# A two-stage graph kernel: the order of a round is rewritten, and the score row is spread through DRAM instead of by TensorE transposes

## The reference

```python
h = maximum(layernorm(x), 0)                    # h0
# stage L0: attention over the adjacency, K = 3 hops
Xw = h @ Wv + bv
e = leaky_relu((Xw @ aw[:d])[:, None, :] + (Xw @ aw[d:])[:, :, None] + ab, 0.2)
alpha = adj * exp(e);  T = alpha / (alpha.sum(-1) + 1e-12)
H = sum over k of (T^k h) @ Wk[k] + bk[k];   x = x + relu(H)
h = maximum(layernorm(x), 0)                    # h1
# stage L1: three graph convolutions
h = relu(adj @ (h @ W1) + b1);  h = relu(adj @ (h @ W2) + b2)
x = x + adj @ (h @ W3) + b3
```

## Time and profile before

| | |
|---|---|
| median of 3 runs (lowest, highest) | 836.76 us (836.75, 837.14) |
| the profiled execution: its time, its span | 837.53 us, 835.4 us |
| busy: PE, DVE, ACT, POOL | 818.7, 718.0, 684.0, 506.8 us |
| share of the span | 98%, 86%, 82%, 61% |
| mean granted TensorE clock | 0.997 |
| DMA moved | 77.54 MB, mean 93 GB/s |

### The profile page before, as it was taken

One profiled execution on the slowest core, in us unless ns is written; L12 is line 12 of the kernel. 1 busy time (PEld: TensorE's weight loads), 2 busy tenths in 40 slices (PEclk: granted clock), 3 DMA queues, 4 the chain that ended last, 5 costly groups with the idle time before them and its releaser, 6 DMA issues.

```text
span 835.4 us, 20996 instructions
## 1 busy us (share of the span) xinstructions
PE 818.7 (98%) x6219; PEld 772.0 (92%) x6219; DVE 718.0 (86%) x2001; ACT 684.0 (82%) x1673; POOL 506.8 (61%) x591
## 2 busy tenths in 40 slices
PE   7899999999999999999999999999999999999996
PEld 6799999999999999999999999999999999999995
DVE  6989889888889889889889889889888889889882
ACT  4788888888888888888888888888888888888774
POOL 3475665665665665665665665665665665665553
PEclk9999999999999999999999999999999999999999
DMA  7144334334344334334334334334334344344101
GB/s 195 43 99 107 86 95 103 91 94 104 88 95 102 92 93 103 92 93 110 84 93 108 87 93 106 87 94 106 88 94 105 85 97 109 83 95 102 46 27 38
DMA packets 245064, 77.54 MB, mean 93 GB/s; under 512 B 202324, under 2 KB 237016, under 8 KB 244952
## 3 DMA queue, kind: packets, MB, share of 16 engines
q1 hardware_dynamic: 243864, 75.16, 37.5%
q10 hardware_dynamic: 1088, 1.05, 0.4%
HBM read 43.39 MB, written 32.77 MB: 91 GB/s over the span
## 4 chain that ended last, share of the span: by engine, by line
PE 95%; ACT 1%; DVE 1%; DMA 1%; issue 1%; POOL 1%; ACTq 0%; DVEq 0%; POOLq 0%
PE bank L984 44%; PE bank_p L984 37%; PE bank_turned L984 7%; PE bank_T L984 5%; PE bank_T L1003 2%; DMA w_raw<-in_L_gnn_Wk 1%; POOL w_p_lo L422 0%; ACT y_full L614 0%; ACT h L490 0%; POOL y__lo L392 0%; PE bank_p L1160 0%; ACT y__hi L614 0%; DVE stats L693 0%; DVE alpha L766 0%; ACT y_hi L569 0%
## 5 line engine op out<-in xcount | busy, mean ns | idle before, releaser
L392 POOL TENSOR_TENSOR y__lo<-y_full,y__hi 128x256 fp32r<-128x256 f32 x256 | 183.6, 737 | 131.4 <-ACT y_full L614 131.4
L383 POOL TENSOR_TENSOR rstd<-veps,minus_half 128x2 f32<-128x2 f32 x128 | 111.6, 872 | 184.9 <-DVE veps L710 184.9
L984 PE MATMUL bank_p<-w_p_hi,h0T_hi 128*128 128x258 f32 (+1 forms) x512 | 176.3, 361 | 0.2 <-DVE y_full L795 0.2
L984 PE MATMUL bank_p<-w_p_lo,h0T_hi 128*128 128x258 f32 (+1 forms) x512 | 165.7, 339 | 0.0
L984 PE MATMUL bank_p<-w_p_hi,h0T_lo 128*128 128x258 f32 (+1 forms) x512 | 142.5, 340 | 0.0
L984 PE MATMUL bank<-w_gcn_hi,y__hi 128*128 128x256 f32 x512 | 130.2, 290 | 2.1 <-ACT y__hi L614 1.3
L984 PE MATMUL bank<-w_gcn_lo,y__hi 128*128 128x256 f32 x512 | 123.7, 278 | 0.0
L614 ACT ACTIVATE y__hi<-bank,bias_col 128x256 fp32r<-128x256 f32 x256 | 119.9, 468 | 3.6 <-PE bank L984 3.5
L614 ACT ACTIVATE y_full<-bank,bias_col 128x256 f32<-128x256 f32 x256 | 120.6, 471 | 0.0
L984 PEld LDWEIGHTS bank_p<-w_p_hi,h0T_hi 128*128 128x128 f32 x512 | 97.1, 190 | 6.5 <-issue 0.4
L984 PEld LDWEIGHTS bank_p<-w_p_lo,h0T_hi 128*128 128x128 f32 x512 | 97.6, 191 | 6.0
(11 more groups left out here) (100 smaller groups left out, 2285.4 us busy)
## 6 DMA issues: line engine op xcount, KB each, us to landing
x_in<-in_x SPq DMA_DIRECT2D x64, 256.0 KB, 3.0
x_new<-x_out SPq DMA_DIRECT2D x64, 256.0 KB, 2.2
h_rows<-h SPq DMA_DIRECT2D x61, 256.0 KB, 2.0
h_blocks<-h_rows SPq DMA_DIRECT2D x244, 64.0 KB, 2.6
adj_blocks<-in_adj SPq DMA_DIRECT2D x256, 32.0 KB, 2.0
w_raw<-in_L_gnn_Wk ACTq DMA_DIRECT2D x3, 256.0 KB, 6.9
w_raw<-in_L_gnn_W SPq DMA_DIRECT2D x3, 256.0 KB, 3.5
wv_raw<-in_L_gnn_Wv ACTq DMA_DIRECT2D x1, 256.0 KB, 3.8
```

The source lines that it names most:

```text
L383: pool.tensor_tensor(rstd[n][k % 2][:], veps[n][k % 2][:], minus_half[:], ALU.pow)\
L392: pool.tensor_tensor(y[n][1][:, c], y_full[n][:, c], plain(y[n][0][:, c]), ALU.subtract)\
L984: return pe.matmul(dst, stationary, moving, start=start, stop=stop, skip_group_check=True)
```

## The change

The score row no longer goes over TensorE from round 3 on. SP writes column v of `uv` (4 bytes from each partition and graph, 1 KB in all) to a DRAM row, waits until it has landed, and reads the row back broadcast to 128 partitions (128 KB) into `v_bc`, from which ACT makes the logits. Both DMAs stand at the head of SP's round. All five engines' rounds are written in a new order. On TensorE: p2, ay, z1, z3, p0/p1 of graph 0, s2, p0/p1 of graph 1, z2, m, ap, s3; z1 of a pair thus moves over the round's border. The dummy transposes of the drain rounds are gone. `y1_made` is now signalled per graph, s2 and s3 wait for their low halves chunk by chunk.

```diff
+        v_rows = [nc.dram_tensor(f"v_rows{k}", (G, P), F32, kind="Internal").ap() for k in range(2)]
+        v_bc = slots(2, "v_bc", [P, G, P])
...
+            def write_scores(i, k):
+
+                sp.wait_ge(uv_made, i + 1)
+                if i >= SPREAD_ON_TENSOR + 2:
+                    sp.wait_ge(v_landed[k % 2], scores_seen(i - 2))
+                sp.dma_start(v_rows[k % 2].rearrange("g (n o) -> n g o", o=1), uv[k % 2][:, :, 1:2],
+                             allow_slow_non_contiguous=True).then_inc(v_out[k % 2], 16)
+
+            def read_scores(i, k):
+
+                sp.wait_ge(v_out[k % 2], scores_seen(i))
+                if i >= SPREAD_ON_TENSOR + 2:
+                    sp.wait_ge(z_made, i - 1)
+                sp.dma_start(v_bc[k % 2][:], v_rows[k % 2].rearrange("(o g) n -> o g n", o=1)
+                             .to_broadcast([P, G, P])).then_inc(v_landed[k % 2], 16)
...
+                spread = here(i, 0) if i >= SPREAD_ON_TENSOR else None
                 if second(i):
                     load_adj_blocks(3, 3)
-                if turned is not None:
+                if spread is not None:
+                    write_scores(i, k)
+                    read_scores(i, k)
+                if second(i):
                     write_rows(turned, turned % ROUND)
                 if (n := here(i, -2)) is not None and not second(i):
-                    load_adj_blocks(n, n % ROUND)
+                    load_adj_blocks(n, n % ROUND, range(2))
+                if turned is not None and not second(i):
+                    write_rows(turned, turned % ROUND)
+                if (n := here(i, -2)) is not None and not second(i):
+                    load_adj_blocks(n, n % ROUND, range(2, P // SQUARE))
+                if (n := here(i, -4)) is not None and after(i, 1):
+                    load_x(n)
...
+                if b is not None and after(i, 3):
+                    pool.wait_ge(y1_lo, b + 1)
+                    adjT_low(b, (k - LAG_B) % ROUND)
+                if c is not None and after(i, 4) and not tail(i):
+                    out_bias(c, (k - LAG_C) % ROUND)
                 if c is not None:
                     y_low(0, c, k - LAG_C)
...
             def logits(i, k):
 
-                act.wait_ge(spread_done, i + 1)
+                if i < SPREAD_ON_TENSOR:
+                    act.wait_ge(spread_done, i + 1)
+                else:
+                    act.wait_ge(v_landed[k % 2], scores_seen(i))
                 act.wait_ge(uv_made, i + 1)
                 if after(i, 2):
                     act.wait_ge(exp_made, i - 1)
                 for g in range(G):
-                    last = act.activation(z[k % 2][:, g, :], spread_ps[:, g, :], ACT.Prelu,
+                    last = act.activation(z[k % 2][:, g, :], (spread_ps if i < SPREAD_ON_TENSOR else v_bc[k % 2])[:, g, :],
+                                          ACT.Prelu,
                                           bias=uv[k % 2][:, g, 0:1], alpha=SLOPE)
                 last.then_inc(z_made, 1)
 
...
+                if b is not None:
+                    y1_high(b, kb)
...
+                if d is not None:
+                    s3_high(d)
...
+                if (n := here(i, -1)) is not None and n > ON_TENSOR + 1:
+                    hT_high(n, n % ROUND)
...
+                if a is not None and a >= SPREAD_ON_TENSOR:
+                    logits(a, k)
+                    exponentials(a, k)
+                if c is not None:
+                    s2_copy(c)
...
                 for g in range(G):
-                    last = dve.scalar_tensor_tensor(y1_full[k % 2][:, g, :], p2_ps[:, g, :],
-                                                    rinv[k % 2][:, g:g + 1], p1[k % 2][:, g, :],
-                                                    ALU.mult, ALU.add)
-                last.then_inc(y1_made, 1)
+                    dve.scalar_tensor_tensor(y1_full[k % 2][:, g, :], p2_ps[:, g, :],
+                                             rinv[k % 2][:, g:g + 1], p1[k % 2][:, g, :],
+                                             ALU.mult, ALU.add).then_inc(y1_made, 1)
 
...
+                if c is not None and after(i, 3):
+                    m_low(c)
+                if b is not None and after(b, 1):
+                    y1_low(b, kb)
...
+                if b is not None:
+                    p0_bias(b, kb)
+                if d is not None and after(d, 1):
+                    s3_low(d)
...
                 if a is not None:
                     attention(a, k)
+                if d is not None:
+                    finish(d, kd)
+                if a is not None and after(i, 2):
+                    p2_low(a, k)
...
-                pe.wait_ge(y1_lo, i + 1)
-                pe.wait_ge(z_made, i + 1)
-                for g in range(G):
-                    for a, b in PARTS:
+                pe.wait_ge(y1_hi, i + 1)
+                pe.wait_ge(z_made, min(i + 1, SPREAD_ON_TENSOR))
+                if after(i, 1):
+                    pe.wait_ge(h_made, i)
+                for a, b in ((HI, HI), (LO, HI), (HI, LO)):
+                    if b == LO:
+                        pe.wait_ge(y1_lo, i + 1)
+                    for g in range(G):
                         last = matmul(ay_ps[:, g, :], aT[k % 2][a][:, g, :], y1[k % 2][b][:, g, :],
-                                      g == 0 and (a, b) == (HI, HI), a == LO)
+                                      g == 0 and (a, b) == (HI, HI), b == LO)
                 last.then_inc(ay_done, 1)
 
             def aggregate(dst, src, i, k):
...
+            def low_by_chunk(n, i, w, dst):
+
+                for c in range(C):
+                    pe.wait_ge(y_lo[n], C * i + c + 1)
+                    for g in range(G):
+                        last = matmul(dst[g], y[n][LO][:, c, g, :], w[HI][:, c, :], False, c == C - 1)
+                return last
+
...
+                for c in range(C):
+                    pe.wait_ge(y_hi[1], C * i + c + 1)
+                    for g in range(G):
+                        for b in (HI, LO):
+                            matmul(dst[g], y[1][HI][:, c, g, :], w_gcn[2][b][:, c, :],
+                                   (g, c, b) == (0, 0, HI), False)
+                low_by_chunk(1, i, w_gcn[2], dst).then_inc(s3_done, 1)
...
+                if i == 2:
+                    z1_product(c)
                 if a is not None:
                     p2_product(a, k, low=False)
-                if i == N_PAIRS:
-                    ay_product(b, kb)
-                if d is not None and not tail(i - 1):
-                    z3_product(d, kd)
-                if b is not None and i < N_PAIRS:
+                if second(i):
                     ay_product(b, kb)
                 if a is not None:
                     p2_product(a, k, low=True)
-                if c is not None:
-                    s2_product(c)
-                if tail(i - 1):
-                    z3_product(d, kd)
                 if first(i):
                     keep_busy(BUSY_SCORES)
-                if a is not None:
+                if i == 2:
+                    ay_product(b, kb)
+                if 1 <= i <= 2:
+                    p01_product(a, k, 0)
+                if i < SPREAD_ON_TENSOR:
                     spread_scores(a, k)
                 if second(i):
                     turn_h(2, 2)
+                if i == 3 or tail(i) and c is not None:
+                    z1_product(c)
+                if b is not None and after(i, 3):
+                    ay_product(b, kb)
+                if c is not None and after(i, 4) and not tail(i):
+                    z1_product(c)
+                if d is not None:
+                    z3_product(d, kd)
+                if a is not None and (first(i) or after(i, 3)):
+                    p01_product(a, k, 0)
+                if c is not None:
+                    s2_product(c)
                 if a is not None:
-                    p01_product(a, k, 0)
                     p01_product(a, k, 1, (0,))
-                if c is not None:
-                    z2_product(c, kc)
                 if first(i):
                     turn_h(1, 1)
                 if a is not None:
                     p01_product(a, k, 1, (1,))
+                if c is not None:
+                    z2_product(c, kc)
+                if b is not None:
+                    m_product(b, kb)
+                if a is not None:
                     ap_product(a, k)
                 if first(i):
                     pe.wait_ge(bias_rows_in, 16 * 2)
                     matmul(bank_3[:, 0:D], ones[:], bk_rows[:], True, True).then_inc(bias_rows_spread, 1)
                     matmul(bank_3[:, D:2 * D], ones[0:1, :], b3_row[:], True, True).then_inc(bias_rows_spread, 1)
                     keep_busy(BUSY_SUMS, bank_2[:, 0:P])
-                if b is not None and tail(i):
-                    keep_busy(BUSY_TAIL, unused)
-                if b is not None:
-                    m_product(b, kb)
```

(64 more changed lines are left out.)

115 lines of the change are left out of this document (69 added, 46 removed).

## The result

The changed kernel takes 1456.68 us (median of 4, 1454.65 to 1462.37) against 836.91 for the kernel before on the same chip (4 runs): ratio 1.7415, 95% interval 1.7379 to 1.7452. The forecast was 817.9, with 812 to 831 as its range. What came is its rival A, a score row that is too late, with a pair of DMAs slower than the 9.1 us that I had as the far end: 12.8.

The account below looks back on a forecast made before the run. TensorE's instruction stream was taken as the bound: 0.31 us saved in each of 61 rounds is 18.9 us, so 837.5 - 18.9 = 818.6 profiled, 817.9 as median. Range 812 to 831.

Parts of the forecast that it names:

- rival A: Logits on ACT: score row comes too late, costing whatever the DMA pair takes over 4.5 us each round; slower, chance 0.13.
- The two DMAs: Score row's write and broadcast read on SP: 2.0 + 2.0 us and 0.05 between, far ends 4.0 and 9.1.
- The fit from which I had 4.3 us for the pair: Score DMAs: skill page's some 2.0 us fixed cost per DMA plus bytes over 436 GB/s, about 4.3 us for both.
- The price rule of rival A: Logits on ACT: each us the DMA pair takes over 4.5 us is paid once a round, over 61 rounds.
- The room of 4.5: Score DMAs: the pair may take about 4.5 us before TensorE waits; from 4.8 the saving is gone.
- Which bound, and what leaves TensorE: TensorE's instruction stream sets the time; its round loses 0.31 us, bounds 0.29 and 0.32.
- The transposes' 0.22: TensorE: removing the score transposes saves 0.14 us and the f32 exit behind them 0.08, each round.
- The 0.08 for one exit less: TensorE: z2 placed directly before m saves one exit from f32, 0.08 us a round.
- rival C: TensorE: z2 before m saves no f32 exit, so only 0.22 us a round goes; 823.4 us, chance 0.08.
- With the durations of crowded engines already: Chains feeding s3, p2 and m: their 0.1 to 0.4 us of room was worked out with durations from already crowded engines.
- B: Low half for s3, y1 for p2 or norm for m slips; at 0.15 us a round, 827 us; chance 0.22.
- Start and drain at zero: Rounds 0 to 2 and the drain: no change in time assumed, with 2 us to either side.

Follow-up runs that it names:

- e3: The changed kernel without the broadcast read; logits wait for the score write and are computed from other data, so not the reference: 1226.97 us.
- e5: The changed kernel without the broadcast read, logits from other data, and the write's 256 single elements put 512 bytes apart in DRAM: 857.83 us.
- e12: The changed kernel with 60 spare transposes a round on TensorE ahead of z2, into a bank that needs no wait: 1354.13 us.
- e16: The changed kernel with v of both graphs written in 128 pieces of 8 bytes, read as 128 KB, and POOL's power before the low half of h: 1034.29 us.
- e8: The changed kernel with u and v of both graphs written as 128 pieces of 16 bytes, and a 2 KB row read broadcast: 926.65 us.
- e13: e8 with POOL's power ahead of the low half of h and, on ACT, the copy of s2 ahead of the logits: 897.42 us.
- e15: e5 with POOL's power ahead of the low half of h; no transposes, no read, logits from other data, so not the reference: 823.92 us.
- e4: The changed kernel without the write; the broadcast read takes 1 KB of input x, so logits come from other data: 858.47 us.

## Why the prediction was wrong, by its own steps

- **The two DMAs: the step that failed.** I took 2.0 + 2.0 and 0.05; they took 7.44 and 5.33, 12.8 together. I knew that no row showed a write of single elements. I took the nearest steady rows, whose write is of 256 KB, and closed the range at 9.1 by two loads, never by a write of small pieces side by side. That the score DMAs are alone was no protection: the write is slow by itself (e3). The Trainium skill (DMA: Bandwidth & Descriptors, Specifications) speaks of read, modify and write below 512 B. Here small pieces alone do not cost the time: e5 has them at 1.6, and only neighbours in DRAM are slow. The fit from which I had 4.3 us for the pair, the Trainium skill (DMA: Bandwidth & Descriptors, Anatomy of one DMA) gives for DMAs that GpSimd issues. SP issues these, and the fit holds no term for the pieces, so it could not warn.
- **The price rule of rival A** (each us over 4.5, once a round, 61 times) is the right kind and a fifth too small: (12.8 - 4.5) x 61 = 506, so 818 + 506 = 1324. Measured 1457. Of the missing 133, 102 are the clock's by e12, and some 30 are not settled. For e16, whose logits start 7.0 after the write's issue, it gives 818 + 155 = 973 for 1034, at a mean clock of 0.938.
- **The room of 4.5.** Not tried: no run had a real row whose logits start less than 5.7 after the write's issue (median of e8 and of e13). e15 has 4.2 without a wait.
- **Which bound, and what leaves TensorE.** The size came right, 0.31 forecast and 0.29 to 0.30 in e15, partly by luck. The transposes' 0.22 is as said. The 0.08 for one exit less is not there: on this, rival C was right. Some 0.07 that the sum did not have came in its place from other products (e15), so C's own 0.22 a round was too little.
- **The clock.** A stall on TensorE was priced at its length. It cost its length, 8.0, and 1.5 to 2.4 us behind it. Together they are 9.5 to 10.4 us, and the round lies 10.4 over e15's 12.24.
- **"With the durations of crowded engines already."** Wrong in one row. The durations were read where DVE's veps stood clear of POOL, and the new order moved it beside POOL's work. Alone this would have made about 858 of the forecast (e4, e5), slower than before and out of my range, with both DMAs hidden. It is also B's kind of failure (norm late for m), at 0.6 a round for the 0.15 that I gave it: e5 and e15 differ by two exchanged steps of POOL and by 34 us.
- **Start and drain at zero.** e15's span is 12.1 us under the earlier trace rows's kernel, where 61 x 0.30 is 18. TensorE is busy 15.4 us less and idle 3.3 more, in the first 120 us and in the drain. So e15's 823.9 lies 6 over the forecast, more than the 2 that I had allowed.

So the direction failed on one number, and a second, smaller one would have turned the sign too.

## What to carry to other kernels

Before a value goes through DRAM on a chain that closes in a round, look at how small the pieces are that stand side by side in the target. Write it with the widest run that a partition can give, or apart, and time that transfer by itself first. When an order is rewritten, list for DVE and POOL what stands beside what, since a duration read in one place is not a duration in another. Count on the starts of blocks, over a whole round, and not on one slow matmul: the cost of leaving an f32 block was an artefact of where a record starts. A stall of 8 us on TensorE cost more than its length here, for what followed it ran at half clock.

## What the runs showed of the hardware

- Writes to DRAM from 128 partitions, to landing: 256 x 4 bytes side by side 7.8 us, the same 512 bytes apart 1.6, the same side by side into an SBUF row 2.0 each for two halves; 256 x 8 bytes 3.0, 128 x 8 bytes 2.9, 128 x 16 bytes 1.4 to 1.9. In the slowest of these the last packet begins 1.12 us after the issue.
- A broadcast read of 1 KB to 128 partitions (128 KB) takes 3.2 alone, 4.0 to 4.2 behind an 8-byte write and 5.2 behind the 4-byte one, though it is issued only when that write has landed. Its first packet begins 0.98 us after the issue alone and 2.6 behind the 4-byte write; why isn't settled.
- DVE's add of a constant to 128x2 ends when a POOL subtraction ends: 0.17 us clear of it, 0.48 and 1.10 beside it in the round shown.
- An f32 matmul of 128x128 takes 0.11 us from its start to the next one's when another f32 one follows; z2's eight take 0.90 ahead of m and 0.80 ahead of an f32r matmul, which then takes 0.32 for 0.235.
- Behind an idle time of 7.6 us, at a granted clock of 0.55, TensorE takes 1.87 us for eight f32 matmuls that take 0.89 otherwise, and the next eight take 1.27 to 1.57 for 0.81. Kept busy with spare work (e12), the same blocks take 1.00 and 0.90.
